# First two token tiles brought forward, first head by halves, new orders of decays and of the end gate

## The reference

```python
xn = (x - mean(x)) / sqrt(var(x) + 1e-5)
q, k, v = silu(xn @ qkv_w.T)              # per head
# blocks of 32 tokens, carried state; equal to one causal product with decay:
attn = sum_m<=n  (q_n . k_m) * exp(-slope_h * (n - m)) * v_m
normed = norm_w * attn * rsqrt(mean(attn**2) + 1e-5)
gate = sigmoid(xn @ gate_w.T)
out = x + (gate * normed) @ out_w.T + xn @ W_base.T + b_base + experts(xn)
```

## Time and profile before

| what | value |
|---|---|
| median of 3 runs | 1080.68 us |
| the profiled execution | 1081.28 us |
| its span, first to last instruction | 1079.5 us |
| TensorE busy | 1073.5 us (99%) |
| ScalarE busy | 702.6 us (65%) |
| VectorE busy | 680.3 us (63%) |
| GpSimd busy | 633.0 us (59%) |
| TensorE's granted clock | at least 0.9 in every slice |

### The profile page before, as it was taken

One profiled execution on the slowest core, in us unless ns is written; L12 is line 12 of the kernel. 1 busy time (PEld: TensorE's weight loads), 2 busy tenths in 40 slices (PEclk: granted clock), 3 DMA queues, 4 the chain that ended last, 5 costly groups with the idle time before them and its releaser, 6 DMA issues.

```text
span 1079.5 us, 19043 instructions
## 1 busy us (share of the span) xinstructions
PE 1073.5 (99%) x5942; PEld 947.2 (88%) x5942; DVE 680.3 (63%) x1150; ACT 702.6 (65%) x1463; POOL 633.0 (59%) x625
## 2 busy tenths in 40 slices
PE   8999999999999999999999999999999999999998
PEld 8998889888898888988898888988889888898898
DVE  6776674656656575665755666465755657566576
ACT  9677565766657665675756766576666756567542
POOL 5548563684737647375544846367473764647654
PEclk9999999999999999999999999999999999999999
DMA  8112020120202101021101102012020211112122
GB/s 301 67 45 83 25 64 21 45 64 26 64 19 64 63 29 58 6 82 39 58 29 44 63 24 63 19 44 63 24 66 16 79 48 43 45 33 75 56 87 79
DMA packets 41606, 60.05 MB, mean 56 GB/s; under 512 B 3936, under 2 KB 21600, under 8 KB 41568
## 3 DMA queue, kind: packets, MB, share of 16 engines
q1 hardware_dynamic: 41280, 59.05, 17.1%
q10 hardware_dynamic: 288, 0.52, 0.1%
HBM read 52.74 MB, written 6.82 MB: 55 GB/s over the span
## 4 chain that ended last, share of the span: by engine, by line
PE 99%; ACT 0%; POOL 0%; DVE 0%; issue 0%; POOLq 0%; DVEq 0%
PE bank_q L1835 8%; PE bank_q L1837 8%; PE bank_q L1836 8%; PE bank_r L1835 6%; PE bank_r L1837 6%; PE bank_r L1836 6%; PE bank_p L1835 6%; PE bank_p L1837 6%; PE bank_p L1836 6%; PE outp L1835 5%; PE outp L1836 5%; PE outp L1837 5%; PE score L1837 3%; PE score L1836 3%; PE score L1835 3%; PE att L1837 3%
## 5 line engine op out<-in xcount | busy, mean ns | idle before, releaser
L419 POOL TENSOR_TENSOR w_lo<-combo,w_hi 128x768 fp32r<-128x768 f32 (+1 forms) x128 | 166.9, 1312 | 148.3 <-ACT w_hi L615 148.3
L419 POOL TENSOR_TENSOR w_lo<-raw,w_hi 128x256 fp32r<-128x256 f32 (+1 forms) x128 | 131.0, 1026 | 130.0 <-ACT w_hi L615 129.5
L1399 DVE TENSOR_TENSOR acc<-acc,outp 128x512 f32<-128x512 f32 x116 | 79.6, 686 | 76.0 <-PE outp L1837 75.1
L470 POOL TENSOR_TENSOR sum_sq<-sum_sq,square 128x512 f32<-128x512 f32 x64 | 82.8, 1294 | 65.9 <-ACT square L771 65.9
L1836 PE MATMUL bank_q<-c_lo,w_hi 128*128 128x512 f32 x276 | 107.4, 389 | 0.0
L1837 PE MATMUL bank_q<-c_hi,w_lo 128*128 128x512 f32 x276 | 107.4, 389 | 0.0
L1835 PE MATMUL bank_q<-c_hi,w_hi 128*128 128x512 f32 x276 | 107.4, 389 | 0.0
L615 ACT ACTIVATE p_hi<-score 128x896 fp32r<-128x896 f32 (+1 forms) x128 | 81.1, 649 | 32.8 <-DVE score L1307 32.1
L1307 DVE TENSOR_TENSOR score<-score,table 128x512 f32<-128x512 f32 (+1 forms) x128 | 75.9, 628 | 40.7 <-PE score L1837 39.8
L1258 DVE TENSOR_TENSOR xs<-bank_r,xs 128x512 f32<-128x512 f32 x64 | 44.2, 691 | 89.1 <-ACT xs L615 61.5
L1835 PE MATMUL outp<-wo_hi,g_hi 128*128 128x512 f32 x250 | 97.6, 390 | 0.0
(11 more groups left out here) (304 smaller groups left out, 3462.7 us busy)
## 6 DMA issues: line engine op xcount, KB each, us to landing
raw<-w_chunks SPq DMA_DIRECT2D x165, 256.0 KB, 2.9
near_dram<-near SPq DMA_DIRECT2D x2, 2048.0 KB, 10.2
table<-near_dram SPq DMA_DIRECT2D x32, 128.0 KB, 2.0
y<-x SPq DMA_DIRECT2D x8, 256.0 KB, 3.3
out<-acc SPq DMA_DIRECT2D x7, 256.0 KB, 2.1
acc<-x SPq DMA_DIRECT2D x6, 256.0 KB, 5.4
acc<-x ACTq DMA_DIRECT2D x2, 256.0 KB, 3.9
hw_dram<-acc SPq DMA_DIRECT2D x1, 512.0 KB, 2.6
```

Source lines behind the costliest of these rows:

```text
L419: pool.tensor_tensor(piece(w_lo[i % 2], j), piece_source(i, j), piece(w_hi[i % 2], j).bitcast(F32), ALU.subtract).then_inc(wlo[j], 1)
L470: pool.tensor_tensor(sum_sq[:, s % 2, :], sum_sq[:, s % 2, :], square[:], ALU.add).then_inc(summed, 1)
L1399: dve.tensor_tensor(tile, tile, outp, ALU.add).then_inc(acc_done, 1)
```

## The change

Six edits. TensorE: twelve multiplications of the identity by itself instead of twenty; only tiles 0 and 1 are turned ahead of `first_head`, and tiles 2 and 3 inside it, behind the first half's products with `b_hi`; k is made by halves of 256 tokens as q was, save its product with the low weights, and the order of the first head's products is by half. VectorE: the second group is measured around `normalise(0)`, and `normalise(1)` comes behind the subtraction of q's low weights. ScalarE: 14 decays ahead of the first weights and five instead of two behind tile 1. In the last body TensorE makes product 7 ahead of `rms(1, 1)` and product 5 behind it.

```diff
--- before.py
+++ after.py
@@ -1159,13 +1159,13 @@
                 act.wait_ge(h_ready, 3 * k + n)
                 copy(h_keep[:, 3 * k:3 * k + n, :].rearrange("p t n -> p (t n)"), routed[k][:, 0:n * (ER + EXPERTS)]).then_inc(h_kept, 1)
 
-            nears(range(17))
+            nears(range(14))
             act.wait_ge(raw_in[0], 32)
             for r in range(2):
                 copy(first_hi[:, 0, 2 * r:2 * r + 2], raw[0][:, 2 * r:2 * r + 2, :]).then_inc(first_whi, 1)
             tokens_hi(0)
             tokens_hi(1)
-            nears(range(17, 19))
+            nears(range(14, 19))
             tokens_hi(2)
             tokens_hi(3)
             nears(range(19, 22))
@@ -1785,14 +1785,17 @@
                 dve.wait_ge(t_hi_done, n)
                 dve.tensor_tensor(c_lo[:, k], t_raw[:, k], c_hi[:, k].bitcast(F32), ALU.subtract).then_inc(t_lo_done, 1)
 
-            for n in range(2):
-                for t in part[n]:
-                    measure(t)
-                variance(n)
+
+            measure(0)
+            measure(1)
+            variance(0)
+            measure(2)
             normalise(0)
-            normalise(1)
+            measure(3)
+            variance(1)
             dve.wait_ge(first_whi, 1)
             dve.tensor_tensor(first_lo[:, 0, 0:2], raw[0][:, 0:2, :], first_hi[:, 0, 0:2].bitcast(F32), ALU.subtract).then_inc(first_qlo, 1)
+            normalise(1)
             for t in range(TB):
                 tokens_lo(t)
             for t in range(TB, NTB):
@@ -2041,9 +2044,9 @@
                     attend(7)
                     more_experts(1)
                     output(10)
+                    prod(G01, 7)
+                    rms(1, 1)
                     prod(G01, 5)
-                    rms(1, 1)
-                    prod(G01, 7)
                     output(11)
                     prod(G01, 3, 4, 2)
                     output(12, 13, 14, 15)
@@ -2159,35 +2162,40 @@
                                        stop=last and kc == KC - 1, skip_group_check=True)
                     return mm
 
-                def k(w_, b_, first, last):
+                def k(tok, w_, b_, first, last):
                     for kc in range(KC):
                         w = slice(kc % 2 * P, kc % 2 * P + P)
-                        mm = pe.matmul(bq, w_[:, 0, 2 + kc // 2, w], b_[:, kc // 2, kc % 2, :], start=first and kc == 0,
+                        mm = pe.matmul(bq[:, tok], w_[:, 0, 2 + kc // 2, w], b_[:, kc // 2, kc % 2, tok], start=first and kc == 0,
                                        stop=last and kc == KC - 1, skip_group_check=True)
                     return mm
 
-                pe.wait_ge(first_whi, 2)
+                halves = slice(0, 256), slice(256, 512)
                 for half in range(2):
                     pe.wait_ge(xh_done, 2 * half + 2)
+                    pe.wait_ge(first_whi, 1)
                     q(half, first_hi, b_hi, True, False)
-                k(first_hi, b_hi, True, False)
-                pe.wait_ge(first_qlo, 1)
-                for half in range(2):
+                    pe.wait_ge(first_qlo, 1)
                     q(half, first_lo, b_hi, False, False)
-                for half in range(2):
+                    pe.wait_ge(first_whi, 2)
+                    k(halves[half], first_hi, b_hi, half == 0, False)
+                    if half == 0:
+
+                        turn_tokens(2)
+                        turn_tokens(3)
                     pe.wait_ge(xl_done, 2 * half + 2)
                     mm = q(half, first_hi, b_lo, False, half == 1)
-                mm.then_inc(first_ready, 1)
-                k(first_hi, b_lo, False, False)
+                    if half == 1:
+                        mm.then_inc(first_ready, 1)
+                    k(halves[half], first_hi, b_lo, False, False)
                 pe.wait_ge(first_wlo, 1)
-                k(first_lo, b_hi, False, True).then_inc(first_ready, 1)
+                k(slice(0, SEQ), first_lo, b_hi, False, True).then_inc(first_ready, 1)
 
 
             pe.wait_ge(consts, 2)
-            for _ in range(20):
+            for _ in range(12):
                 pe.matmul(outp[:, 0:P], ident[:], ident[:], start=True, stop=True, skip_group_check=True)
             pe.wait_ge(consts, CONSTS)
-            for t in range(TB):
+            for t in range(2):
                 turn_tokens(t)
             first_head()
             first_rows(2, 0)
```

## The result

The changed kernel takes 1082.32 us (median of 22 executions, 1082.09 to 1083.19 us), the kernel before 1080.68 us (22 executions, 1080.42 to 1081.57 us). The ratio is 1.0014 with a 95% interval of 1.0008 to 1.0020: slower by 1.6 us, within the 0.2% that I had called no difference, but outside the range that I gave (up to 1081.6 us). The profiled execution took 1083.19 us, with a span of 1081.4 us; it is one of five in 22 in which the granted clock, the mean over the execution (1.000 is 2.4 GHz throughout), was 0.998 instead of 1.000 (1082.65 to 1083.19 us); the other 17 took 1082.09 to 1082.39 us.

The account below looks back on a forecast made before the run. TensorE was taken as the bound, busy 1073.5 us of a 1079.5 us span. Front +0.4 us and tail -0.35 us on the profiled 1081.28 us gave 1081.33 us, as a median 1080.7 us, range 1079.7 to 1081.6 us.

Parts of the forecast that it names:

- The join: Second batch's last turn on TensorE, just 0.5 us behind VectorE's last normalised tile; said to decide the case.
- The tail: Last body, products 7 and 5 swapped: removes TensorE's wait behind output(11), -0.35 us, bounds 0 and -0.35 us.
- The first tile: VectorE's normalising of tile 0 in the front: ready at 7.96 us, 0.9 us sooner.
- its turn: TensorE's transposes of tile 0, starting at 8.0 us.
- the power held up by `first_lo`: GpSimd's second power beside VectorE's subtraction of q's low weights: 0.45 us longer, bounds 0 and 0.55 us.
- the decays cost nothing: ScalarE, five decays instead of two ahead of tile 2: 0.9 us more, no cost, since ScalarE would wait anyway.
- The twelve multiplications: TensorE's remaining idle multiplications of the identity at the start, 24 records, ending at 7.5 us.
- VectorE's new order: Front: tiles 0 and 1 ready at 7.96 and 8.42 us, tiles 2 and 3 at 12.05 and 12.5 us.
- the front: Start of the kernel to the second batch's last turn, 22.77 instead of 22.35 us: +0.4 us, bounds 0.0 and +0.5 us.
- The median's baseline: Sum taken from the profiled 1081.28 us, then carried to the median, 0.60 us lower: 1080.68 + 0.05 us.
- rival (c): TensorE's clock left at 1.2 GHz in the front's waits, delaying tokens_hi(3) by 1.6 to 2.1 us: 1082.8 us, chance 0.08.

Follow-up runs that it names:

- experiment 2: Changed kernel with GpSimd's subtraction of k's low weights held back until tiles 2 and 3 are normalised; 1081.32 us, ratio 1.0003.
- experiment 3: Changed kernel with seven more identity multiplications on TensorE ahead of the turn of tile 2; 1082.42 us, ratio 1.0014.
- experiment 9: Kernel before with sixteen idle multiplications instead of twenty; 1080.56 us, ratio 0.9997.
- experiment 5: Kernel before with twelve idle multiplications instead of twenty, nothing else; 1081.37 us, ratio 1.0004.
- experiment 6: Kernel before with products 7 and 5 swapped, twelve idle multiplications, and ScalarE's copy of the second load ahead of three decays; 1080.30 us, ratio 0.9997.
- experiment 7: Changed kernel with the decays in their old order, 17 ahead of the first weights and two behind tile 1; 1082.40 us, ratio 1.0015.
- experiment 8: Changed kernel with twenty idle multiplications again instead of twelve; 1082.42 us, ratio 1.0015.
- experiment 4: Changed kernel with q's low weights subtracted behind normalise(1), and TensorE's order q high, k high, turns, q low; 1081.07 us, ratio 1.0002.
- experiment 11: Changed kernel with GpSimd's k subtraction held back until tiles 2 and 3 are normalised and ScalarE's second-load copy ahead of tokens_hi(2); 1080.85 us, ratio 0.9998.
- experiment 10: Kernel before with products 7 and 5 swapped, ScalarE's second-load copy ahead of three decays, and sixteen idle multiplications; 1080.25 us, ratio 0.9993.

## Why the prediction was wrong

**Right.** The join was named: the last turn decides, and it did in all 13 kernels. The tail was -0.35 us forecast and -0.34 us measured. The first tile (7.96 us forecast, 7.84 us), its turn (8.0 us, 7.99 us), the power held up by `first_lo` (+0.45 us forecast; +0.51 us measured) and that the decays cost nothing came as written. The twelve multiplications ended at 7.90 us, not 7.5 us, where their last record only starts; that cost nothing.

**The step that failed: "VectorE's new order".** It read that VectorE "waits for the power, refines and normalises tiles 2 and 3", with 0.6 us for the refinement. The same paragraph had weighed the sharing of a port between the two engines for the power, and did not ask what GpSimd does next. Its k subtraction had waited for `first_qlo` behind VectorE's last normalisation before the change; `first_qlo` now comes ahead of the refinement, so the subtraction starts with it. The step took 1.23 us instead of 0.16 us, 1.07 us that experiment 2 gives back nearly whole (1.0 us in the median). Tiles 2 and 3 were ready at 12.90 and 13.36 us instead of the forecast 12.05 and 12.5 us, and the front is +1.38 us, as experiment 3 shows it without the clock's fall, instead of +0.4 us. The bounds of the term, 0 and 0.55 us, were the bounds of one meeting out of two. The Trainium skill, SBUF — State Buffer, section "Who interferes with whom", has the rule for both: the second port pair is locked for the whole instruction, and a VectorE instruction with two SBUF inputs takes part in it. The trace agrees: the step ended 0.02 us behind GpSimd's subtraction (11.94 and 11.92 us).

**The median's baseline.** I set the sum against a profile with its last turn at 22.35 us, and carried it to the median as if its front were the usual one. That term, a front carried over at its full size, is the second one that failed. The profiled front was not the usual one: its multiplications had run late. The difference to the median, 0.60 us, is the front's own; a median execution has its last turn near 21.7 us (experiment 9). Of the changed kernel, whose 17 executions without a fall of the clock lie within 0.3 us, this can't be taken off again. So the account of the medians is +1.38 (front) + 0.60 (baseline) - 0.34 (tail) = +1.64 us, and 1082.32 - 1080.68 = 1.64 us. This is bookkeeping and no test of its own, since front and baseline are read from the same profile of before; what it says is that of the 1.6 us by which the forecast missed, 1.0 us is the meeting and 0.6 us the baseline.

**The clock, rival (c).** It happened, in five of 22 executions, but for less: 0.87 us in the profiled one, not 1.6 to 2.1 us, because the fall came at 14.8 us and behind the turns, and 0.45 of the 1.32 us by which it delays the gate rows are covered by the late second batch. "It decides if the rise comes later than about 10 us" was the wrong form of it; the clock rose by 8.0 us and fell again. For the median it is nothing. What the trace of before showed, that 0.8 us of wait leave the clock up, says nothing of 1.5 us of wait behind others.

**Where the gain went.** What was to be won, tile 0 one microsecond sooner, is real, and TensorE's turn of it starts 1.6 us earlier than before (7.99 against 9.63 us). But the chain that sets the last turn goes through tile 3, the second load and the third power, and tile 3 was moved back by 2.6 us (12.36 + 1.00 against 10.80 us). The reordering served the head of the chain that was not the bound.

**Open.** Why seven executions of 11 lost the clock in experiment 5, three in experiment 6, two in experiment 7 and five of 22 in the changed kernel, but none in experiments 3 and 8 and none of 33 in experiments 2, 4 and 11, is shown as a pattern (fewer multiplications ahead of the turns, or a longer wait for tile 2 with nothing in it, more falls) and not as a rule. I did not try an order of VectorE that keeps tile 3 where it was and still brings tile 0 forward.

The fastest kernel of all is experiment 10: 1080.25 us, with ten of its 11 executions below the lowest of the 27 of before beside it (1080.39 us). Against their median the ratio's interval still reaches 1.0002, since the kernel before itself spreads over 1.2 us, so the interval alone doesn't show it to be faster.

## What to carry to other kernels

When an instruction is moved on one engine, follow the semaphore it tells to the other engines' queues: what it lets start sooner may be the long operation that collides with the short steps on the critical chain. Bringing the first piece forward is worth nothing if the join behind waits for the last piece; write down what the join waits for, and cost the move there. And before a profile's times are set against a median, look whether its own excess over the median lies in the part that is changed.

## What the hardware showed that I had not expected

- A VectorE step on 128x2 elements with SBUF inputs waited out a whole GpSimd subtraction (1.23 instead of 0.16 us); the GpSimd power on 128x2 took 1.21 us next to a VectorE subtraction of two SBUF tiles, 0.70 us alone.
- The clock fell in five of 22 executions of the same kernel. In the traced one it was at 1.2 GHz for 3.4 us, though TensorE was never idle for longer than 1.49 us after its first work; what stood before the fall were waits and the turns of two tiles.
- The clock rises at another time in each execution: at 5.2 to 8.6 us in the 13 traces here (from there on the records start 0.11 us apart instead of 0.21 us), with TensorE's first work at 2.4 us in all. Twenty multiplications of the identity ended at 9.8 to 10.1 us in the three traces that have them, with rises at 7.9 to 8.6 us; with a rise at 5.2 us they would end near 8.1 us, an estimate from these spacings. Sixteen took the kernel's spread from 1.2 us down to 0.2 us.
- The first tile landed at another time too: VectorE's first statistics start at 3.95 to 4.75 us in the traces, and the whole front moves with them (0.69 us in experiment 7).
